# A graph attention network's gather stream: the pacing waits taken off GpSimd's gathers, and its index copies joined and moved

## The chip, the cores and the metric

One Trainium2 chip, one of its cores. The metric is the time of one execution on the device in microseconds (us); the number compared is the median over several executions. A profile is one further execution, recorded by the hardware's profiler, with a time of its own.

## The reference

A graph of 6,250 nodes with 32 channels and 106,250 directed edges (self loops among them), sorted by destination. Three GATv2 attention layers with 8 heads, each followed by a residual and a batch normalization over the nodes, then one equivariant layer and layer norms. Cut to one attention layer:

```
xl, xr = (x @ Wl + bl), (x @ Wr + br)            # [N, 8, 32]
e      = leaky_relu(xl[src] + xr[dst], 0.2)
logits = einsum('ehc,hc->eh', e, att)
p      = exp(logits - segment_max(logits, dst)[dst])
alpha  = p / (segment_sum(p, dst)[dst] + 1e-16)
out    = segment_sum(xl[src] * alpha, dst).mean(heads) + bias
x      = batchnorm(leaky_relu(out, 0.01) + x)
```

Layer 4 (the "second network") gathers wide rows of the nodes by `src`, forms messages from edge vectors and a small radial network, and adds them up by `dst`.

## The kernel before

**Steps.** The edges are cut into 468 steps of 256 edges (two columns `t` of 128, one edge on each partition), ordered so that all edges of a step belong to one block of 128 destination nodes. A step k of attention passes these stages, each on an engine with its own queue, tied by semaphores that count steps:

- GpSimd gathers the source rows by two indirect DMAs (L506), one for each column, from `table` in HBM into `xg[:, s % 6, t, 96:128]`. `xg` has six slots. The numbers of the rows lie in `idx`, a ring of 12 slots that GpSimd itself fills by small copies from `srci` (`number`, L483), one a column.
- VectorE makes the transposed one-hot `oht` of the destinations (L1150), five steps ahead of its own main work.
- TensorE's `front` (L610, L613) transposes the gathered rows into PSUM and multiplies the destination rows in by `oht`. It runs four steps ahead of TensorE's `aggregate`. ScalarE copies the result to `xt` (L830).
- TensorE's `zed` (L622, L624) multiplies by the weights, two steps ahead.
- VectorE applies the leaky relu and the attention weights (`u`, L1155), sums over channels (`lr`, L1163; this bumps `r_done`), and every third step adds the linear part to the logits (L1169).
- GpSimd's `keep_rows` (L491) copies the gathered rows of step k-3 (`LAG`) out of `xg` into `xs`, which holds two groups of rows.

**Groups.** 48 steps are a group; a layer has ten, the last with 36 steps. When a group's logits are complete, the running maxima over segments are made (`running`, `maxima`: two scans, L1257 and L1258, and a chain of short instructions between VectorE, TensorE and ScalarE). Only then can the group's rows be weighed (`px`, L1182), multiplied by a one-hot (`aggregate`, L637) and added to `acc` (L1196). This second half of group g-1 runs interleaved with the first half of group g, on the same three engines. So group 0 of a layer has only first halves, and a last stretch has only second halves. Inside `maxima` VectorE makes the one-hots of the next group's first steps (`early_places`), and TensorE their fronts (`early_fronts`), one by one between the links of the chain.

**Order on GpSimd.** `attention_body` runs 12 steps. For step k it waits that the slot is free: `front_done` of step k-6 and `xs_done` of step k-6. Before the first gather it also waits for the one-hot of step k-3 (`oht_done`, L501), before the second for the channel sums of step k-8 (`r_done`, the `else` branch, L503); before each for its own number (`idx_done`, L504). Behind each gather it copies one column's numbers for step k+1, and behind both the rows of step k-3. `then()` is a counter's increment and does no other work.

**SP** loads the destinations' places `dr` (L424) three steps at a time, once the one-hots that read the old ones are done.

Of the kernel before, what the change touches and what calls it, by code (L numbers as in the profile page):

```python
# [32 lines left out]
N, C, H, LAYERS, E = 6250, 32, 8, 3, 106250  # L33
# [5 lines left out]
S6 = 6  # L39
BODIES = 8  # L40
GS = S6 * BODIES
NBODIES = 2 * -(-(PAIRS + BLOCKS - 1) // (2 * S6))
GROUPS = -(-NBODIES // BODIES)
LASTB = NBODIES - (GROUPS - 1) * BODIES
NS = NBODIES * S6
# [14 lines left out]
ZS = SELF + NS  # L60
QS = NS // J + SELF
AGGS = NS + GROUPS + 1
NUMBERS = 2 * NS + 2
LAG = 3
AHEAD = 8
WIDE = 8 + 8 * 5
# [12 lines left out]
def gatv2_program(nc, x, src, dst, edge_w, edge_v, Wl, bl, Wr, br, att, conv_bias, gamma, beta,  # L79
# [3 lines left out]
    with ctx:  # L83
        def sb(name, shape, dt=F32):
            return ctx.enter_context(nc.sbuf_tensor(name, shape, dt))

        def sem(name):
            return ctx.enter_context(nc.semaphore(name))
# [21 lines left out]
        srci = sb("srci", [P, NSP, 2], I32)  # L110
# [20 lines left out]
        idx = sb("idx", [P, 2 * S6, 2], I32)  # L131
# [158 lines left out]
        r_done = sem("r_done")  # L290
        lin_done = sem("lin_done")
        l_done = sem("l_done")
        oht_done = sem("oht_done")
# [6 lines left out]
        idx_done = sem("idx_done")  # L300
# [160 lines left out]
        def _(pool):  # L461
# [15 lines left out]
            def then():  # L477

                pool.sem_inc(passed, 1)

            def number(k, s, t):

                nc.gpsimd.tensor_copy(idx[:, s, t:t + 1], srci[:, bass.ds(k, 1), t]).then_inc(idx_done, 1)  # L483

            rowsets = xs[:].rearrange("p g s q c -> p (g s) q c")

            def keep_rows(t, to, s):

                pool.wait_ge(gat[s], 32 * t + 32)
                then()  # L490
                nc.gpsimd.tensor_copy(to, xg[:, s, :, 96:128]).then_inc(xs_done, 1)  # L491

            def attention_body(l, i, starts):
                k0 = i * 2 * S6
                for s in range(2 * S6):

                    pool.wait_ge(front_done, AHEAD + l * ZS + k0 + s + 1 - S6)
                    pool.wait_ge(xs_done, AHEAD + l * NS + k0 + s + 1 - S6)
                    for t in range(2):
                        if t == 0:  # L500
                            pool.wait_ge(oht_done, AHEAD + l * NS + k0 + s + 1 - 3)  # L501
                        else:
                            pool.wait_ge(r_done, AHEAD + l * ZS + k0 + s + 1 - 8)  # L503
                        pool.wait_ge(idx_done, AHEAD + l * NUMBERS + (k0 + s) * 2 + t + 1)  # L504
                        then()
                        nc.gpsimd.indirect_dma_start(  # L506
                            out=xg[:, s % S6, t, 96:128], out_offset=None, in_=table,
                            in_offset=bass.IndirectOffsetOnAxis(ap=idx[:, s, t:t + 1], axis=0)).then_inc(gat[s % S6], 16)
                        number(k0 + s + 1, (s + 1) % (2 * S6), t)
                    if s >= LAG or not starts:  # L510
                        to = rowsets[:, bass.ds((k0 + (2 * GS + s - LAG)) % (2 * GS), 1), :, 0:C].rearrange("p o q c -> p (o q) c") \
                            if not starts else rowsets[:, s - LAG, :, 0:C]
                        keep_rows(l * NBODIES + i * 2 + (s - LAG) // S6, to, (s - LAG) % S6)

            pool.sem_inc(xs_done, AHEAD)
            pool.sem_inc(idx_done, AHEAD)
# [3 lines left out]
            with pool.Fori(0, LAYERS) as l:  # L520
                pool.wait_ge(x_new, l + 1)
                then()
                nc.gpsimd.memset(acc[:], 0.0).then_inc(acc_done, 1)
                for t in range(2):
                    number(0, 0, t)
                pool.wait_ge(tab_new, 16 * (l + 1))
                then()
                attention_body(l, 0, True)
                with pool.Fori(1, NBODIES // 2) as i:
                    attention_body(l, i, False)  # L530
                for s in range(S6 - LAG, S6):
                    keep_rows((l + 1) * NBODIES - 1, rowsets[:, (NS - S6 + s) % (2 * GS), :, 0:C], s)

                pool.wait_ge(f_g, l + 1)
                then()
                with pool.Fori(0, SELF // 2) as i:
                    for r in range(2):
                        m = l * SELF + i * 2 + r
                        pool.wait_ge(gb_done, AHEAD + m - 1)
                        nc.gpsimd.tensor_tensor(  # L540
                            xp[:, r].rearrange("p b (h c) -> p b h c", h=H),
                            xn[:, bass.ds(i * 4 + 2 * r, 2), :].unsqueeze(2).to_broadcast([P, 2, H, C]),
                            gate[:, 3, bass.ds(i * 4 + 2 * r, 2), :].unsqueeze(3).to_broadcast([P, 2, H, C]),
                            ALU.mult).then_inc(xp_done, 1)
# [11 lines left out]
            def numbers1(k, half):  # L556

                pool.wait_ge(pa_done, HELD + k + 3 - S6)
                nc.gpsimd.tensor_copy(idx[:, 3 * half:3 * half + 3, :], srci[:, bass.ds(k, 3), :]).then_inc(idx_done, 1)
                pool.wait_ge(idx_done, AHEAD + LAYERS * NUMBERS + k // 3 + 1)  # L560

# [1053 lines left out]
```

## Time and profile before

| | |
|---|---|
| median of 3 runs | 7,853.58 us (7,843.77 to 7,854.25) |
| the profiled execution | 7,840.21 us |
| its span, first to last instruction | 7,838.1 us |
| granted clock of TensorE, mean | 0.793 of full speed |
| GpSimd busy | 4,875.5 us, 62% |
| VectorE busy | 6,394.4 us, 82% |
| TensorE busy (matmul) | 6,163.7 us, 79% |

How to read it: PE is TensorE, PEld its weight loads, DVE VectorE, ACT ScalarE, POOL GpSimd, SP the queue that issues most loads. The three attention layers take about 1,920 us each, from 208 to 5,960 us; what follows is the equivariant layer. Busy times leave out waits on semaphores. "issue" as a releaser means that the profile shows nothing that the engine waited for. An idle time stands with the instruction behind it and with what ended it.

### The profile page before, as it was taken

The numbers are of one execution on the slowest core, as the hardware profiler recorded it, in microseconds if no ns is written. First come the engines' busy times: TensorE is split into PE (matmuls) and PEld (weight loads), VectorE is DVE, ScalarE is ACT, GpSimd is POOL, SyncE is SP. The second block draws the span as 40 slices with busy tenths as digits, with TensorE's granted clock in tenths as the row PEclk, the third lists the DMA queues.
The fourth block names the chain that finished last, engine by engine and source line by source line (L and its number), as shares of the span: only waits on it lengthen the run. The fifth ranks groups of instructions, "written<-read, shape, count | busy, mean of one in ns | idle before, by whom it ended". The sixth has DMA issues, their size and how long they took to land.

```text
span 7838.1 us, 176242 instructions
## 1 busy us (share of the span) xinstructions
PE 6163.7 (79%) x26512; PEld 4656.6 (59%) x26513; DVE 6394.4 (82%) x12894; ACT 3281.8 (42%) x11055; POOL 4875.5 (62%) x8226
## 2 busy tenths in 40 slices
PE   0688888885478888888547888888854999999998
PEld 0366666664446666655435656665544888888887
DVE  7688888885468888888547888888846999999999
ACT  0255545553125545445313545444511444444444
POOL 1888878870288878885038878887412555555554
PEclk8899999998599999999759999999965555555555
DMA  2211111110011111111001111111101111111111
GB/s 87 49 34 33 37 31 34 34 30 0 9 36 34 37 31 34 33 36 22 0 15 36 36 32 34 33 36 31 19 0 31 30 30 30 30 30 30 30 30 28
DMA packets 214500, 237.82 MB, mean 30 GB/s; under 512 B 72973, under 2 KB 195854, under 8 KB 213902
## 3 DMA queue, kind: packets, MB, share of 16 engines
q1 hardware_dynamic: 93582, 163.43, 7.2%
q0 software_dynamic: 120704, 72.40, 6.9%
q14 instruction: 185, 1.52, 0.1%
q8 instruction: 29, 0.48, 0.0%
HBM read 222.34 MB, written 13.20 MB: 30 GB/s over the span
## 4 chain that ended last, share of the span: by engine, by line
issue 27%; DVE 22%; PE 21%; POOL 12%; DVEq 11%; DMA 3%; POOLq 3%; ACT 1%; ACTq 0%; SPq 0%
POOL xg L506 7%; PE psum L637 6%; PE psum L622 6%; POOL idx L483 4%; DVE xs L1525 3%; PE psum L715 2%; DVEq L1510 2%; DVE acc L1537 2%; DMA xg<-table,idx 2%; DVEq L1189 2%; DVEq L990 2%; DVE u L1155 2%; PE psum L705 2%; PE psum L610 2%; PE psum L624 1%
## 5 line engine op out<-in xcount | busy, mean ns | idle before, releaser
L506 POOL DMA_INDIRECT xg<-table,idx x2808 | 2877.3, 1025 | 754.4 <-issue 278.0
L622 PE MATMUL psum<-wz,xt 128*128 x5928 | 1820.5, 401 | 51.2 <-ACT xt L890 49.7
L637 PE MATMUL psum<-px,oh 128*128 128x272 f32 x5616 | 1632.5, 414 | 161.2 <-DVE acc L1196 80.6
L819 ACT ACTIVATE dist<-iota_f,ndloc 128x128 f32<-128x128 f32 x2808 | 974.2, 394 | 1512.5 <-PE psum L637 1500.6
L637 PEld LDWEIGHTS psum<-px,oh 128*128 128x128 f32 x5616 | 961.7, 191 | 516.0 <-DVE acc L1196 210.8
L622 PEld LDWEIGHTS psum<-wz,xt 128*128 128x128 f32 x5928 | 1024.4, 197 | 384.6 <-ACT lin L837 72.5
L771 PE MATMUL psum<-w2e,xt 65*128 65x256 f32 x1872 | 1056.6, 668 | 228.7 <-DVE xs L1525 175.3
L552 POOL DMA_INDIRECT xg<-table,idx x936 | 905.4, 967 | 384.5 <-issue 242.2
L1163 DVE TENSOR_REDUCE lr<-u 128x16 f32<-128x512 f32 x1482 | 1012.8, 686 | 158.7 <-DVE u L1155 117.3
L1182 DVE TENSOR_TENSOR px<-xs,pg 128x528 f32 (+1 forms) x1404 | 997.1, 710 | 109.0 <-issue 47.7
L1155 DVE SCALAR_TENSOR_TENSOR u<-psum,atts 128x512 f32<-128x512 f32 x1482 | 1017.3, 686 | 71.0 <-PE psum L624 69.2
L624 PE MATMUL psum<-bz,ones_b 96*128 x2964 | 839.7, 283 | 0.0
L610 PE MATMUL psum<-ident,xg 128*128 128x128 f32 x2808 | 589.0, 293 | 263.3 <-DMA xg<-table,idx 243.5
L772 PEld LDWEIGHTS psum<-w2e,xt 65*128 65x128 f32 x1872 | 630.0, 337 | 169.0
L1196 DVE TENSOR_TENSOR acc<-acc,psum 128x272 f32 x1404 | 606.1, 432 | 121.8 <-issue 100.0
L830 ACT COPY xt<-psum 128x256 f32<-128x256 f32 x1404 | 524.1, 373 | 416.1 <-PE psum L613 252.2
L1150 DVE TENSOR_SCALAR oht<-dr,iota_p 128x256 bf16<-128x256 bf16 x1404 | 439.4, 315 | 298.7 <-PE psum L613 252.2
L483 POOL COPY idx<-srci 128x1 int32 (+1 forms) x2814 | 661.4, 235 | 16.0
L610 PEld LDWEIGHTS psum<-ident,xg 128*128 128x128 f32 x2808 | 362.0, 149 | 515.5 <-issue 339.7
L540 POOL TENSOR_TENSOR xp<-xn,gate 128x512 f32 x78 | 81.8, 1051 | 934.9 <-DVEq L990 934.9
L771 PEld LDWEIGHTS psum<-w2e,xt 65*128 65x128 f32 x1872 | 504.2, 329 | 246.2 <-DVE u L1519 183.6
L613 PE MATMUL psum<-oht,x 128*96 128x256 bf16 x1404 | 429.4, 306 | 263.4 <-issue 248.4
(270 smaller groups left out, 8379.7 us busy)
## 6 DMA issues: line engine op xcount, KB each, us to landing
dr<-dlocs SPq DMA_DIRECT2D x468, 192.0 KB
xg<-table,idx POOLq DMA_INDIRECT x3744
at<-w_rows SPq DMA_DIRECT2D x156, 192.0 KB
fl<-flags SPq DMA_DIRECT2D x30, 576.2 KB
flags<-fl SPq DMA_DIRECT2D x10, 576.2 KB, 3.1
table<-xn SPq DMA_DIRECT2D x3, 784.0 KB, 3.6
xp<-keys SPq DMA_DIRECT2D x5, 385.0 KB, 4.5
u<-keys SPq DMA_DIRECT2D x5, 385.0 KB, 4.4
```

Source lines behind the costliest of these rows:

```text
L483: nc.gpsimd.tensor_copy(idx[:, s, t:t + 1], srci[:, bass.ds(k, 1), t]).then_inc(idx_done, 1)
L506: nc.gpsimd.indirect_dma_start(out=xg[:, s % S6, t, 96:128], out_offset=None, in_=table, in_offset=bass.IndirectOffsetOnAxis(ap=idx[:, s, ...
L552: nc.gpsimd.indirect_dma_start(out=feat[:, s, e, 8:8 + WIDE], out_offset=None, in_=table1, in_offset=bass.IndirectOffsetOnAxis(ap=idx[:, s ...
L610: pe.transpose(xt_ps(r)[:, e * P:(e + 1) * P], xg[:, s, e, :], ident[:])
L622: pe.matmul(out_z, xt[:, r, e * P:(e + 1) * P], wz[:, bass.ds(l, 1), :].rearrange("p o z -> p (o z)"), start=True, stop=False)
L624: last = pe.matmul(out_z, ones_b[:], bz[:, bass.ds(l, 1), :].rearrange("p o z -> p (o z)"), start=False, stop=True)
L637: last = pe.matmul(agg_ps(r), oh[:, r, e, :], px[:, r, e, :], start=(e == 0), stop=(e == 1))
L771: pe.matmul(z_ps(r, 0, HC)[:, e, :], rows, w2e[:, 0:HC], start=True, stop=True)
L819: last = op.activation(dist[:, e, :], iota_f[:], ACT.Abs, bias=ndloc[:, bass.ds(k, 1), e])
L1155: op.scalar_tensor_tensor(u[:, r], z_ps(r, 0, HC), 0.0, atts[:, bass.ds(l, 1), :].to_broadcast([P, 2, HC]), ALU.max, ALU.mult).then_inc(u_ ...
L1163: op.tensor_reduce(lr[:, c, j], u[:, r].rearrange("p e (h c) -> p e h c", h=H), AX.X, ALU.add).then_inc(r_done, 1)
L1182: op.tensor_tensor(px[:, r, :, 0:H * C1].rearrange("p e (h c) -> p e h c", h=H), rows.unsqueeze(2).to_broadcast([P, 2, H, C1]), pg[:, 2 * ...
```

## The change

Four edits, all on GpSimd's queue and within the attention layers:

1. The two waits `oht_done` (step k-3) and `r_done` (step k-8) before the gathers are gone; a gather waits for its slot, and for the number.
2. `number` copies both columns of a step at once, 128x2 in place of 128x1, so `idx_done` counts steps and not columns (`NUMBERS`).
3. It does so for step k+2 and behind the step's second gather; the numbers of steps 0 and 1 are copied ahead of the loop.
4. `keep_rows` of step k-3 stands between the step's two gathers and no longer behind both.

```
-NUMBERS = 2 * NS + 2
+NUMBERS = NS + 2
...
-            def number(k, s, t):
+            def number(k, s):
-                nc.gpsimd.tensor_copy(idx[:, s, t:t + 1], srci[:, bass.ds(k, 1), t]).then_inc(idx_done, 1)
+                nc.gpsimd.tensor_copy(idx[:, s, :], srci[:, bass.ds(k, 1), :].rearrange("p o t -> p (o t)")).then_inc(idx_done, 1)
...
                     pool.wait_ge(front_done, AHEAD + l * ZS + k0 + s + 1 - S6)
                     pool.wait_ge(xs_done, AHEAD + l * NS + k0 + s + 1 - S6)
+                    pool.wait_ge(idx_done, AHEAD + l * NUMBERS + k0 + s + 1)
                     for t in range(2):
-                        if t == 0:
-                            pool.wait_ge(oht_done, AHEAD + l * NS + k0 + s + 1 - 3)
-                        else:
-                            pool.wait_ge(r_done, AHEAD + l * ZS + k0 + s + 1 - 8)
-                        pool.wait_ge(idx_done, AHEAD + l * NUMBERS + (k0 + s) * 2 + t + 1)
                         then()
                         nc.gpsimd.indirect_dma_start(...)
-                        number(k0 + s + 1, (s + 1) % (2 * S6), t)
-                    if s >= LAG or not starts:
-                        to = ...
-                        keep_rows(l * NBODIES + i * 2 + (s - LAG) // S6, to, (s - LAG) % S6)
+                        if t == 0 and (s >= LAG or not starts):
+                            to = ...
+                            keep_rows(l * NBODIES + i * 2 + (s - LAG) // S6, to, (s - LAG) % S6)
+                    number(k0 + s + 2, (s + 2) % (2 * S6))
...
-                for t in range(2):
-                    number(0, 0, t)
+                for s in range(2):
+                    number(s, s)
```

## Rows read from the trace of the kernel before

**Rows 1.** The page: busy time by engine; VectorE and GpSimd in 40 slices.
```profile
PE 6163.7 (79%) x26512; PEld 4656.6 (59%) x26513; DVE 6394.4 (82%) x12894; ACT 3281.8 (42%) x11055; POOL 4875.5 (62%) x8226
...
DVE  7688888885468888888547888888846999999999
...
POOL 1888878870288878885038878887412555555554
```

**Rows 2.** Waits, whole span: waiter, releaser, us in total, times, longest.
```profile
POOL xg L506 <- DVE oht L1150: 274.1, 34, 11.9
...
DVE oht L1150 <- PE psum L613: 252.2, 279, 5.2
...
PE psum L610 <- DMA xg<-table,idx: 243.5, 153, 98.3
```

**Rows 3.** Timeline of GpSimd, two steps inside a group: start, duration, instruction.
```profile
1207.29 0.97 POOL L506 DMA_INDIRECT xg<-table,idx  x1 [0.16 <-issue]
1208.26 0.19 POOL L483 COPY idx<-srci 128x1 int32 x1
1208.62 0.98 POOL L506 DMA_INDIRECT xg<-table,idx  x1 [0.16 <-POOL idx L483]
1209.60 0.20 POOL L483 COPY idx<-srci 128x1 int32 x1
1209.72 0.24 POOL L491 COPY xs<-xg 128x64 f32 x1
1210.12 0.98 POOL L506 DMA_INDIRECT xg<-table,idx  x1 [0.16 <-issue]
```

**Rows 4.** Timeline of GpSimd at two boundaries of groups, one group apart.
```profile
2450.06 0.96 POOL L506 DMA_INDIRECT xg<-table,idx  x1 [10.13 <-DVE oht L1150]
...
2607.82 0.96 POOL L506 DMA_INDIRECT xg<-table,idx  x1 [11.13 <-DVE oht L1150]
```

**Rows 5.** Waits in layer 2's groups 1 to 9 (2300 to 3672 us).
```profile
DVE oht L1150 <- PE psum L613: 34.8, 50, 2.4
...
DVE px L1182 <- POOL xs L491: 8.1, 13, 0.8
...
DVE px L1182 <- PE psum L637: 4.4, 9, 0.9
...
PE psum L610 <- DMA xg<-table,idx: 17.7, 24, 1.8
...
POOL xs L491 <- DMA xg<-table,idx: 2.1, 1, 2.1
```

**Rows 6.** Windows: busy us by engine inside a middle group; in group 0.
```profile
2461.00:2600.00 139.00, 126.59 (x605) 90.38 (x603) 122.06 (x246) 75.25 (x283) 119.71 (x223) 0.98 0.17 36
2155.30:2286.30 131.00, 93.95 (x420) 53.15 (x418) 79.41 (x156) 25.39 (x94) 115.79 (x230) 0.99 0.19 38
```

**Rows 7.** Waits in layer 2's group 0 (2150 to 2286 us).
```profile
DVE oht L1150 <- PE psum L613: 47.7, 42, 3.0
...
POOL xg L506 <- issue: 9.9, 52, 1.8
```

**Rows 8.** GpSimd in the equivariant layer: a six-column copy's group; gathers back to back.
```profile
L559 POOL COPY idx<-srci 128x6 int32 x156 | 29.1, 186 | 556.3 <-DVE u L1519 469.0 <-DVEq L1486 87.3
...
6999.04 0.96 POOL L552 DMA_INDIRECT xg<-table,idx  x1 [0.31 <-issue]
7000.31 1.05 POOL L552 DMA_INDIRECT xg<-table,idx  x1 [0.30 <-issue]
```

**Rows 9.** Durations in ns (min/median/max) in 2300 to 3672 us; groups with their means.
```profile
L483 POOL COPY idx<-srci x829: 187/195/781, 2300.9 to 3661.5; 128x1 int32 x166
...
L1150 DVE TENSOR_SCALAR oht<-dr,iota_p x416: 272/286/666, 2300.5 to 3659.9; 128x256 bf16<-128x256 bf16 x139
...
L1182 DVE TENSOR_TENSOR px<-xs,pg x419: 696/700/817, 2301.7 to 3670.6; 128x528 f32 x104, 128x528 f32<-128x528 f32 x36
...
L1182 DVE TENSOR_TENSOR px<-xs,pg 128x528 f32 (+1 forms) x1404 | 997.1, 710 | 109.0 <-issue 47.7
...
L1150 DVE TENSOR_SCALAR oht<-dr,iota_p 128x256 bf16<-128x256 bf16 x1404 | 439.4, 315 | 298.7 <-PE psum L613 252.2
```

More of the change, by code:

```diff
@@ L508, in attention_body @@
                             in_offset=bass.IndirectOffsetOnAxis(ap=idx[:, s, t:t + 1], axis=0)).then_inc(gat[s % S6], 16)
-                        number(k0 + s + 1, (s + 1) % (2 * S6), t)
-                    if s >= LAG or not starts:
-                        to = rowsets[:, bass.ds((k0 + (2 * GS + s - LAG)) % (2 * GS), 1), :, 0:C].rearrange("p o q c -> p (o q) c") \
-                            if not starts else rowsets[:, s - LAG, :, 0:C]
-                        keep_rows(l * NBODIES + i * 2 + (s - LAG) // S6, to, (s - LAG) % S6)
+                        if t == 0 and (s >= LAG or not starts):
+                            to = rowsets[:, bass.ds((k0 + (2 * GS + s - LAG)) % (2 * GS), 1), :, 0:C].rearrange("p o q c -> p (o q) c") \
+                                if not starts else rowsets[:, s - LAG, :, 0:C]
+                            keep_rows(l * NBODIES + i * 2 + (s - LAG) // S6, to, (s - LAG) % S6)
+                    number(k0 + s + 2, (s + 2) % (2 * S6))
             pool.sem_inc(xs_done, AHEAD)
```

## The prediction

> **What bounds the kernel now.** I began with the page's totals and its slices [rows 1]. In the attention layers (slices 2 to 29) GpSimd and VectorE are both busy for eight tenths and more, and TensorE has the next largest total, so no total names the bound, and the waits have to. In the waits of the whole span [rows 2], GpSimd stands 274.1 us before a gather because of a one-hot (L1150), in only 34 places; TensorE stands 243.5 us for rows that a gather has not landed, 98.3 of them once at the first layer's start; VectorE stands 252.2 us before the one-hot, because the front step (L613) of TensorE is late. So gathers are held back in one place and missed in another.
>
> The timeline of GpSimd shows where [rows 3, 4]. Between group boundaries it never rests: a step takes 2.83 us (1207.29 to 1210.12), nearly all of it two gathers and three copies. At a boundary it rests 10.13 and 11.13 us [rows 4], since a gather waits for the one-hot of three steps before, which VectorE issues only inside the running maxima. From 2450.06 to 2607.82, one group of 48 steps, GpSimd needs 157.8 - 11.1 = 146.7 us, 3.05 a step.
>
> That does not make GpSimd the bound of a whole group. In one layer's groups 1 to 9 (420 steps, 1,370 us) VectorE stood for a late front 34.8 us, and for TensorE's aggregate 4.4 us; TensorE stood for gathers 17.7 us [rows 5]. VectorE is busy 122 of 139 us in a mid-group stretch [rows 6], and most of the remaining 17 us are not the gathers' fault (34.8 / 9 = 3.9 a group is). Group 0 is different: it has no weighing and no sums, VectorE is busy 79 of 131 us and stood 47.7 us for fronts, while GpSimd's pauses before gathers are the short ones of dispatch but for one of 1.8 us [rows 6, 7]. I read this as: GpSimd sets the pace of group 0; in groups 1 to 9 VectorE does, with GpSimd so near that its lateness shows now and then.
>
> **The change part by part.**
>
> *The number copies.* Now a step is gather (0.97), copy (0.19), gap to the next gather (0.17), gather (0.98), copy, row copy that begins 0.12 later, gap: 2.83 us [rows 3]. In the trace each copy begins as the gather before it ends, and a gather begins 0.16 us after the copy before it. The new order is gather, row copy, gap, gather, one number copy, gap: 0.97 + 0.24 + 0.16 + 0.98 + 0.19 + 0.16 = 2.70. The two-column copy isn't in the trace; a copy of six columns took 186 ns against 195 for one [rows 8], so I price it as one. The saving is 0.13 us a step, not the 0.35 (0.19 and its gap) of a whole copy, because the second copy lay beside the row copy, and now each stands alone. Bounds: nothing, if the row copy waits; 0.35, if all gaps close. Nothing may close entirely: two gathers with no copy between them are still 0.30 apart [rows 8].
> In group 0 this is on the path: 48 x 0.13 = 6.2 us, in three layers 19 us (bounds 0 and 50). In groups 1 to 9 it only adds to GpSimd's lead.
>
> *The two waits.* What stays is the free slot: gather k waits for front k-6 (and the row copy, long done). TensorE runs its front four steps ahead of its own aggregate, so front k-6 is done well before the old waits end at a boundary: gathers to step 101 can go at once, while today those from 99 wait until 2450.06. That is three steps, 8.5 us of GpSimd's work, moved into the rest of 10 to 11 us. GpSimd's demand for a group falls from 146.7 to 146.7 - 48 x 0.13 = 140.5 us against a period of 157.8, so it enters with a lead near six steps and keeps most of it. A front is then late by nothing but a rare landing, so what falls away is VectorE's wait for fronts. Three layers of 34.8 make 104 us; I take 90 of it, since some of the waits may hide others that end just after (bounds 50, and 130 with 4.4 x 3 for aggregates and small pauses the view does not list). The initial 98.3 us are the layer's start and stay.
>
> *Contention.* GpSimd will work beside VectorE at other moments. What a copy can cost: the row copy is given as releaser of VectorE's product (L1182) for 8.1 us, 13 times [rows 5]; that product takes 700 ns at the median and 696 at best, the one-hot 286 and 272, with 666 at worst [rows 9]. So today's loss is near nothing for the product and at most 0.05 us a step for the one-hot. I take 5 us of loss for the 27 boundaries, where GpSimd newly works beside the scans. The bounds are a gain of 41 us (1,404 one-hots by 29 ns, what their mean of 315 lies over the median [rows 9]) and a loss of one row or number copy a step, 0.19 us. The Trainium skill, "SBUF — State Buffer" (the diagram's reading of the engine ports), has the pair of ports shared by GpSimd and VectorE as an exclusive lock: an instruction with two SBUF inputs, or in a 2-port mode, and a GpSimd instruction that reads SBUF block each other whole, and who starts first keeps the other out. The trace agrees on the direction seen from GpSimd (a number copy takes 195 ns at the median and 781 at worst) and shows almost none of it from VectorE's side. By that rule alone the saved copy could give VectorE back up to 0.19 us a step; by the product's row it gives nothing, and the sum goes by the row.
>
> *Moved past.* The row copy now stands in front of the second gather, and waits for the rows of step k-3. It does so 1.3 us sooner after their issue than today. Today it waited for a landing once in that layer's stretch, 2.1 us [rows 5], after some three steps (8.5 us); then it will be two steps and one gather (6.5 us). Behind it on GpSimd's queue stand the second gather and everything after; with six steps of lead I price it at nothing, and 2 x 3 us if the rare late ones recur. No DMA of SP is moved; its loads of places still hang on the one-hots.
>
> *Sum.* 7,840 (the profiled execution's own time; span 7,838) - 19 - 90 + 5 = 7,736. The runs' median, 7,853.6, lies 13 above the profiled one; I forecast 7,748 against it.
>
> **The rivals.**
>
> *GpSimd really sets every group's pace.* Then a group shrinks by both its rest and the copies: 157.8 to 140.5, 17 us, eight times, with 6 for group 0 and 36 x 0.13 = 5 for the last one: about 147 a layer, 441 in all, 7,412. For it: GpSimd never rests within a group, and the fronts' slack is small. Against it: VectorE, which has the maxima to do at every boundary besides its steps, stood only 3.9 us a group for fronts. Some of its other pauses might be consequences of lateness I don't see; so values between 7,650 and 7,412 belong here.
>
> *The release does nothing.* If the free slot comes no sooner than the old waits in the run of a group, and the lead taken at the boundary is lost by its middle, late fronts return in the second half. Then half of the 90 stays and group 0 gives its 19, or less: 7,854 - 19 - 15 = 7,820, with a span from 7,800 to 7,850. For it: today's lead from the boundary is used up within the group, or TensorE would not have stood for gathers 24 times in nine groups [rows 5]. Against it: GpSimd's demand, 140.5, is well under the period.
>
> *Slower: copies that block VectorE's products.* With the slots alone as release, GpSimd's step hangs on the front's end, and so keeps a fixed place against VectorE's step. If in that place the row or the number copy holds the product off for its whole length every step, it costs 1,404 x 0.19 = 267 us less the 104 gained: 8,017. It decides from 104 / 1,404 = 0.07 us a step on. The page cited above speaks for this one. Against it: at today's changing phase the product's mean is 710 ns against a median of 700 [rows 9], though GpSimd works nearly all the time, so most phases do no harm.
>
> **How the numbers follow.** The forecast has 0.66, GpSimd as the bound 0.12, a release without effect 0.13, slower 0.09. The forecast's own bounds are 7,854 - 50 - 130 - 41 = 7,633 and 7,854 - 0 - 50 + 5, about 7,810; I take 7,640 to 7,825, which also takes in half of the rival without effect and leaves the first and the last outside. A measurement of this kernel tells a difference of 0.2% (16 us) from none. Faster than that are the forecast, the first rival and some two thirds of the second, 0.86; within it the rest of the second, and a mild form of contention, 0.06; slower 0.08.
>
> **What would show it.** In the profile after, GpSimd's long waits before a gather should name the front (L613) instead of L1150; its total wait should grow to some 10 to 17 us a group, spread over it; its step without waits should be 2.70. TensorE's waits for gathers in groups 1 to 9 and VectorE's for fronts there should be near zero, and those of group 0 fall by 6 us a layer. The distance between scans (L1257), a group's period, should go from about 158 to 154. If that distance falls by over 8 us, VectorE was not the bound and the first rival holds. If L1182 or L1150 is longer, or waits for GpSimd, the last one does. If VectorE's waits for fronts vanish and the distance stays, the waits only hid something else that ends at the same moment, and my step from a wait to a gain is what fails.

## The result, and the profile after

The changed kernel takes 7,585.5 us (median of 4 runs, 7,582.3 to 7,587.4) against 7,848.7 for the kernel before beside it (7,833.2 to 7,854.3): 0.9667 of the time, 95% interval 0.9651 to 0.9684. That is 263 us less, where 105 were forecast, and outside the range of 7,640 to 7,825. The profiled execution took 7,587.1 us, span 7,585.0, at a granted clock of 0.79 as before. The times in the text on groups and steps below are worked out from starts in the traces; from the gather on, lines are lower by 4 (L506 is L502, L610 is L606, L613 is L609, L637 is L633, L1150 is L1146, L1182 is L1178, the scan L1257 is L1253).

The page after, busy time by engine and the same two rows of slices as in [rows 1]:

```profile
PE 6116.2 (81%) x26512; PEld 4596.1 (61%) x26513; DVE 6316.2 (83%) x12894; ACT 3414.8 (45%) x11055; POOL 4623.7 (61%) x6822
...
DVE  7699989985479989988458899989738999999999
...
POOL 1888878850288788873158788878013555555554
```

GpSimd is busy 252 us less, VectorE 78 less. In the attention layers VectorE's digits go from eight to nine, GpSimd's stay at eight.

Where the 253 us of the span went is told by the distances between starts: from the first to the last `u` (L1151, before L1155) of group 0, 128.1 us became 122.0, in three layers 18 us; from scan to scan, in what follows the length of a group, 158.2 became 149.3, 24 times, 213 us; the last such distance of a layer went from 138.2 to 131.0, three times, 22 us. 18 + 213 + 22 = 253.

Waits of the whole span after, as in [rows 2] (waiter, releaser, us in total, times, longest):

```profile
POOL xg L502 <- PE psum L609: 276.6, 35, 12.4
...
PE psum L606 <- DMA xg<-table,idx: 187.9, 60, 98.9
...
DVE oht L1146 <- PE psum L609: 142.2, 134, 4.9
...
POOL xs L491 <- DMA xg<-table,idx: 17.3, 7, 3.1
```

GpSimd rests as long as before (276.6 against 274.1 us) but now for the front's slot. TensorE's waits for gathers fall by 56 us, VectorE's for fronts by 110.

GpSimd's timeline after, inside a group, as in [rows 3], and at two boundaries one group apart, as in [rows 4]:

```profile
2300.08 0.98 POOL L502 DMA_INDIRECT xg<-table,idx  x1 [0.16 <-POOL idx L483]
2301.07 0.24 POOL L491 COPY xs<-xg 128x64 f32 x1
2301.47 0.98 POOL L502 DMA_INDIRECT xg<-table,idx  x1 [0.16 <-POOL xs L491]
2302.46 0.19 POOL L483 COPY idx<-srci 128x2 int32 x1
2302.81 1.38 POOL L502 DMA_INDIRECT xg<-table,idx  x1 [0.16 <-POOL idx L483]
...
2353.99 0.98 POOL L502 DMA_INDIRECT xg<-table,idx  x1 [11.12 <-PE psum L609]
...
2503.21 0.98 POOL L502 DMA_INDIRECT xg<-table,idx  x1 [11.11 <-PE psum L609]
```

A step is 2.73 us (2,300.08 to 2,302.81) where 2.70 were forecast and 2.83 were before. A group now takes 149.2 us from boundary to boundary, 11.1 of it rest: 138.1 of work, where 140.5 were forecast.

Waits in layer 2's groups 1 to 9 after (2,211 to 3,504 us), as in [rows 5]; no row there has TensorE waiting for a gather:

```profile
POOL xg L502 <- PE psum L609: 91.5, 11, 12.3
...
DVE px L1178 <- PE psum L633: 14.7, 42, 0.4
...
DVE px L1178 <- POOL xs L491: 6.6, 9, 0.8
...
POOL xs L491 <- DMA xg<-table,idx: 5.9, 3, 2.8
...
DVE oht L1146 <- PE psum L609: 0.6, 2, 0.4
```

VectorE's waits for fronts fell from 34.8 us to 0.6, as forecast; the eleven rests of GpSimd are what is left.

Windows inside a middle group and in group 0 (start:end, length, busy us of PE, PEld, DVE, ACT and POOL with their instructions, clock, DMA share, GB/s), as in [rows 6]:

```profile
2364.00:2500.00 136.00, 125.46 (x606) 86.97 (x604) 124.55 (x252) 80.36 (x281) 113.41 (x180) 1.00 0.18 37
2079.60:2195.00 115.40, 86.41 (x386) 49.68 (x384) 72.48 (x143) 23.22 (x86) 101.48 (x170) 0.97 0.20 41
```

VectorE is busy 91.6% of the stretch inside a group (87.8% before), TensorE 92.3% (91.1%), GpSimd 83.4% (86.1%). In group 0 VectorE still stands for fronts, 45.9 us between 2,060 and 2,196 us where [rows 7] has 47.7; the prediction had these waits fall by 6 us a layer.

The chain of work that ended last, cut to the same groups, is a view that the prediction doesn't use. First the kernel before (2,300 to 3,672 us), then after (2,211 to 3,504 us); the view cuts its line at the end:

```profile
by line: issue 28.6%; PE psum L637 12.2%; POOL xg L506 10.2%; PE psum L622 9.8%; POOL idx L483 6.5%; DMA xg<-table,idx 4.2%; PE psum L610 3.0%; PE psum L613 2.6%; PE psum L624 2.5%; DVEq L1189 2.1%; DVE u L1155 1.9%; POOLq L491 1.3%; DVE ac
```

```profile
by line: PE psum L633 26.2%; PE psum L618 22.3%; issue 9.4%; DVE u L1151 6.2%; PE psum L620 5.3%; PE psum L606 4.8%; DVEq L1185 3.7%; DVE acc L1192 2.5%; PE psum L609 2.4%; DVE px L1178 1.4%; DVEq L1178 1.4%; DVEq L986 1.4%; DVE oht L1146 1
```

Before, a fifth of the chain in just those groups ran through gathers, number copies and landings (10.2 + 6.5 + 4.2). After, none of the named lines is GpSimd's; TensorE's products and the path through VectorE are.

How early the rows come is a plainer test. Worked out from the traces, groups 1 to 8: from the end of a step's second gather to its front's first transpose (L610) it is never under 1.5 us in the kernel before, and 2.1 to 2.7 us at the median in 21 of a group's last 24 steps. So there the front starts almost as soon as the rows are in. After, the least of all is 8.3 us: TensorE has the rows long before it takes them.

Groups with their means after, as in [rows 9]:

```profile
L1178 DVE TENSOR_TENSOR px<-xs,pg 128x528 f32 (+1 forms) x1404 | 992.1, 707 | 95.8 <-PE psum L633 60.5 <-POOL xs L491 20.4 <-issue 8.4
...
L1146 DVE TENSOR_SCALAR oht<-dr,iota_p 128x256 bf16<-128x256 bf16 x1404 | 405.2, 290 | 181.2 <-PE psum L609 142.2 <-issue 21.7
```

### The profile page after: what moved, and what is told of

Its sections match the earlier page's. It is cut to its first block, busy times and chain, and to the rows that moved or that the text cites. A ratio compares the mean times of both kernels' runs of the same rounds, so it can differ in the third digit from the quotient of the medians.

```text
span 7585.0 us, 170428 instructions
## 1 busy us (share of the span) xinstructions
PE 6116.2 (81%) x26512; PEld 4596.1 (61%) x26513; DVE 6316.2 (83%) x12894; ACT 3414.8 (45%) x11055; POOL 4623.7 (61%) x6822
## 4 chain that ended last, share of the span: by engine, by line
PE 37%; DVE 26%; issue 18%; DVEq 14%; POOL 3%; DMA 1%; ACT 1%; POOLq 1%; ACTq 0%; SPq 0%
PE psum L633 14%; PE psum L618 12%; DVE u L1151 4%; DVE xs L1521 4%; PE psum L620 3%; DVEq L1185 3%; PE psum L711 2%; DVEq L1506 2%; PE psum L606 2%; DVE acc L1533 2%; DVEq L986 2%; DVE acc L1192 2%; PE psum L701 2%; POOL xg L502 2%; DVE u L1515 1%
## 5 line engine op out<-in xcount | busy, mean ns | idle before, releaser
L502 POOL DMA_INDIRECT xg<-table,idx x2808 | 2874.0, 1024 | 733.3 <-PE psum L609 276.6
L618 PE MATMUL psum<-wz,xt 128*128 x5928 | 1842.0, 404 | 102.7 <-ACT lin L833 51.7
L633 PE MATMUL psum<-px,oh 128*128 128x272 f32 x5616 | 1650.9, 417 | 158.5 <-DVE acc L1192 121.8
L633 PEld LDWEIGHTS psum<-px,oh 128*128 128x128 f32 x5616 | 959.6, 190 | 572.2 <-DVE acc L1192 362.2
L618 PEld LDWEIGHTS psum<-wz,xt 128*128 128x128 f32 x5928 | 966.6, 195 | 550.0 <-ACT lin L833 218.6
L1178 DVE TENSOR_TENSOR px<-xs,pg 128x528 f32 (+1 forms) x1404 | 992.1, 707 | 95.8 <-PE psum L633 60.5
L1151 DVE SCALAR_TENSOR_TENSOR u<-psum,atts 128x512 f32<-128x512 f32 x1482 | 1014.3, 684 | 68.4 <-PE psum L620 68.4
L833 ACT COPY lin<-psum 128x16 f32<-128x16 f32 x1482 | 255.2, 172 | 1316.7 <-DVE u L1151 1316.1
L606 PE MATMUL psum<-ident,xg 128*128 128x128 f32 x2808 | 579.6, 289 | 192.2 <-DMA xg<-table,idx 187.9
L606 PEld LDWEIGHTS psum<-ident,xg 128*128 128x128 f32 x2808 | 369.1, 149 | 402.8 <-issue 244.0
L819 ACT ACTIVATE oh<-dist 128x256 f32<-128x256 f32 x1404 | 585.6, 417 | 44.3
L768 PE MATMUL psum<-w2e,xt 65*128 65x128 f32 x1872 | 593.4, 421 | 0.0
```

The costliest lines, as they stand in the source:

```text
L502: nc.gpsimd.indirect_dma_start(out=xg[:, s % S6, t, 96:128], out_offset=None, in_=table, in_offset=bass.IndirectOffsetOnAxis(ap=idx[:, s, ...
L606: pe.transpose(xt_ps(r)[:, e * P:(e + 1) * P], xg[:, s, e, :], ident[:])
L618: pe.matmul(out_z, xt[:, r, e * P:(e + 1) * P], wz[:, bass.ds(l, 1), :].rearrange("p o z -> p (o z)"), start=True, stop=False)
L633: last = pe.matmul(agg_ps(r), oh[:, r, e, :], px[:, r, e, :], start=(e == 0), stop=(e == 1))
L768: last = pe.matmul(psum[:, 4 + r, e * P:(e + 1) * P], rows, w2e[:, HC:HC + P], start=True, stop=True)
L1151: op.scalar_tensor_tensor(u[:, r], z_ps(r, 0, HC), 0.0, atts[:, bass.ds(l, 1), :].to_broadcast([P, 2, HC]), ALU.max, ALU.mult).then_inc(u_ ...
```

## The experiments

Theory A was the prediction's, VectorE paces groups 1 to 9 and lateness costs what the waits show. Theory B: before, GpSimd's own time and the rest that it must take make the group; after, something else does, a floor that no group goes below. The expectations call B the lateness theory (runs 1 to 4), the theory of GpSimd's pace (5 to 8) and the floor model (from 9 on). A rival beside both is their copy theory: the second number copy slows VectorE's instructions.

**1 to 4, beside one another (the kernel before: 7,850.7 us).** The waits away alone is the kernel before less these lines:

```
-                        if t == 0:
-                            pool.wait_ge(oht_done, ...)
-                        else:
-                            pool.wait_ge(r_done, ...)
```

> The kernel before with the two pacing waits taken off the gathers, and nothing else: two number copies a step, one step ahead, the row copy behind both gathers. Lateness theory: a group of the changed kernel takes 149.3 us between scans because no front waits for rows any more; that floor belongs to VectorE and TensorE, and GpSimd meets it whenever its work and its rest at the boundary are below it. Here they are 146.7 us and a small rest, so groups 1 to 9 fall from 158.2 to 149 to 151 us, group 0 stays (first channel product to last 128 us); 7,610 to 7,650 us. Copy theory (it was the second number copy, beside VectorE's instructions, that cost the groups their time): groups stay above 154 us, 7,740 or more.

Measured: 7,681.9 us, ratio 0.9792 (0.9776 to 0.9808). A group takes 152.0 us, group 0 128.4. That is above the lateness theory's 149 to 151 and 7,650, and below the copy theory's 154 and 7,740: two copies a step cost the groups 2.7 us at most here, and neither range was met. The lead that GpSimd wins at the boundary is used up again: from the second gather's end to the front it is over 14 us in the first six steps and 2.3 in the last. The copies alone is the changed kernel with those four lines back.

> The changed kernel with both pacing waits put back: joined number copies, two steps ahead, the row copy between the gathers. Lateness theory: GpSimd needs 48 x 2.86 = 137 us and rests 11 us at the boundary, 148 together, just under the floor, so groups come to 149 to 152 us and group 0 to 122; 7,600 to 7,650 us. Copy theory: nearly the whole gain too, 7,590 to 7,620. If the waits themselves matter at every step (the free slot comes sooner than they do), groups stay at 155 or more and the time above 7,720 us.

Measured: 7,595.7, ratio 0.968 (0.9664 to 0.9696), a group 149.3, group 0 121.7, the last one 133.6. It lies 4 us under the lateness theory's range and inside the copy theory's, so this run doesn't part the two. With the new copies the release is worth some 10 us (the two ratios' intervals overlap), and the copies alone give all of the gain in groups 1 to 8. The third is the changed kernel with the row copy behind both gathers and the number copy:

```
-                        if t == 0 and (s >= LAG or not starts):
-                            ... keep_rows(...)
                     number(k0 + s + 2, (s + 2) % (2 * S6))
+                    if s >= LAG or not starts:
+                        ... keep_rows(...)
```

> The changed kernel with the row copy back behind both gathers (right behind the number copy); the rest as changed. GpSimd's step: 0.97 + 0.31 + 0.97 + 0.13 + 0.24 + 0.16 = 2.78 us against 2.70, so group 0 takes 48 x 0.08 = 4 us more a layer, and groups 1 to 9 stay at 149.3 by the lateness theory: 7,585 + 12 = 7,597 us. By the copy theory, where a copy stands matters to VectorE in each step: more than 30 us either way.

Measured: 7,611.8, ratio 0.9701 (0.9685 to 0.9717), a group 150.1, group 0 123.4. GpSimd's timeline and VectorE's one-hot in this kernel:

```profile
2300.08 0.99 POOL L502 DMA_INDIRECT xg<-table,idx  x1 [0.30 <-issue]
2301.08 0.19 POOL L483 COPY idx<-srci 128x2 int32 x1
2301.21 0.24 POOL L491 COPY xs<-xg 128x64 f32 x1
2301.60 0.98 POOL L502 DMA_INDIRECT xg<-table,idx  x1 [0.15 <-issue]
2302.89 0.95 POOL L502 DMA_INDIRECT xg<-table,idx  x1 [0.30 <-issue]
...
L1146 DVE TENSOR_SCALAR oht<-dr,iota_p 128x256 bf16<-128x256 bf16 x1404 | 478.1, 342 | 186.3 <-PE psum L609 147.5 <-issue 21.5
```

The two copies overlap here, but the gathers behind one another stand 0.30 us apart, so the step (2,300.08 to 2,302.89, gather to same gather) is 2.81 us against 2.73. And the one-hot's mean is 342 ns against 290, 1,404 x 52 ns = 73 us of VectorE's time. The kernel is 26 us slower than the changed one, of which 3 x 1.4 are group 0's; how the rest divides isn't isolated. 12 us had been expected, or over 30 by the copy theory; it is neither.

The fourth leaves the second gather of each step out, and the waits for landings count one gather a step; the second column's source rows stay zero, so that part of the attention's result is not computed.

```
-                    for t in range(2):
+                    for t in range(1):
```

> The changed kernel without its second gather in the attention steps (the second column's source rows stay zero, the output is not the reference's): GpSimd's step falls from 2.7 to about 1.5 us. Lateness theory: the floor of 149.3 us a group is VectorE's and TensorE's, so groups 1 to 9 stay within 1 us of it, and only group 0 falls, from 122 us to about 95 to 105 (TensorE was busy 94 of 131 us there): 7,500 to 7,535 us. If GpSimd still bounds the groups after the change, or its instructions slow VectorE's, they fall below 147 us, and the time below 7,470.

Measured: 7,470.8, ratio 0.9521 (0.9505 to 0.9537). A group stays at 150.0, as expected. Group 0 falls to 80.6 us, lower than the 95 to 105 expected, and with it the whole time. GpSimd's wait in this kernel, whole span:

```profile
POOL xg L502 <- PE psum L609: 1837.6, 982, 17.4
```

With half of the gathers and rests in 982 places, a group is no shorter: some 149.3 us is a floor that isn't GpSimd's, and the changed kernel stands on it. Only group 0 still hung on GpSimd.

**5 to 8 (the kernel before: 7,867.9 us).** In the kernel before, TensorE has idle time with no releaser ("issue") just before L613, where the block number is loaded into a register behind the wait for a gather. Rows of the kernel before, then of after, in the stretches of [rows 5]:

```profile
PEld psum L613 <- issue: 114.7, 217, 1.0
...
PE psum L613 <- issue: 60.2, 141, 0.7
```

```profile
PEld psum L609 <- issue: 15.8, 51, 0.8
...
PE psum L609 <- issue: 2.5, 7, 0.4
```

The fifth loads the number ahead of the wait, in the kernel before, and the eighth does in the changed one (the fronts at a group's start excepted):

```
+                b = pe.value_load(brow[0:1, bass.ds(k, 1)], ...)
                 pe.wait_ge(gat[s], 32 * t + 32)
...
-                b = pe.value_load(brow[0:1, bass.ds(k, 1)], ...)
```

> The kernel before, and in TensorE's front the load of the block number stands ahead of the wait for the gathered rows (but for the early fronts), not between the transposes and the one-hot's matmul. Before, TensorE stood 60 us a layer before that matmul (L613) for nothing that the profile names, in groups 1 to 9, and the changed kernel 2.5 us. Theory of GpSimd's pace: those pauses only fill time until the next rows land; a group lasts as long as GpSimd's work plus its rest (145.7 + 11.7 = 157.4 us), whatever TensorE does in it; the time falls by no more than 25 us. Theory of the exposed load: late rows cost the time of a load that the sequencer can no longer do ahead, 6.4 us a group; then it falls by 100 to 170 us, to 7,680 to 7,750.

Measured: 7,833.7, ratio 0.9957 (0.9941 to 0.9974), 34 us less, where 25 at most were expected by the theory of GpSimd's pace and 100 by the other; a group 157.9, and the profiled span 9 us less than before's. TensorE's waits in this kernel, in the same stretch of 2,300 to 3,672 us (the gather's wait is at L612, the one-hot's product at L616):

```profile
PE psum L612 <- DMA xg<-table,idx: 75.6, 106, 2.1
...
PE psum L616 <- issue: 2.5, 7, 0.4
```

Before, the two rows were 17.7 [rows 5] and 60.2, 77.9 in sum; now 75.6 and 2.5, 78.1 in sum. A group shrank by 0.4 us. The "issue" before L613 had been the gather's lateness under another name.

> The changed kernel with the same early load of the block number in TensorE's front. Rows are 5.6 us early there in groups 1 to 8, so nothing waits for the load in them: 7,585 us, within 10. If TensorE bounds the changed groups (it has the largest share of the chain that ended last, 37%), it may fall by 20 us or more.

Measured: 7,582.0 (7,579.3 to 7,583.8), ratio 0.9636 (0.962 to 0.9652); a group 149.3, group 0 120.8. Of the kernels that compute the whole result it is the fastest, but only 3 us under the changed kernel, beside a kernel before that took 19 us more; nothing to tell apart.

The sixth has the joined numbers two steps ahead alone (waits kept, rows behind both gathers); the seventh only moves the row copy between the gathers, in the kernel before.

> The joined number copies, two steps ahead, and nothing else: both pacing waits kept, the row copy behind both gathers (behind the number copy). GpSimd's step with the waits gone and this order was 2.87 us (active 2.56 and a gap of 0.31 between gathers). Theory of GpSimd's pace: 48 x 2.87 + 11.7 = 149.5 us a group, so 150 to 151; with group 0 at 123 us 7,615 to 7,650 us in all. If the place of the row copy is what gives the gain, it stays above 7,750 us.

Measured: 7,615.8, ratio 0.9679 (0.9663 to 0.9695), a group 150.1, group 0 123.7.

> The kernel before, with the row copy moved from behind both gathers to between them (behind the first column's number copy); both number copies and both waits kept. GpSimd's step: still two gathers, a lone number copy and a pair of number and row copy, 2.83 us. Theory of GpSimd's pace: no change, within 20 us of before. If the place of the row copy matters by itself (it meets VectorE elsewhere), more than 50 us.

Measured: 7,873.7, ratio 1.0003 (0.999 to 1.0015), a group 159.9. So the joined copy, two steps ahead, carries the change; its two parts were not tried apart. The row copy's place is worth nothing by itself. Where the numbers are joined it is worth 26 us between run 3 and after, and 20 between runs 6 and 2, whose ratios are the same, so that this second one isn't shown.

**9 to 18: more GpSimd work, and less.** If B holds, copies that nobody reads (`spare`) bring the old group time back, in proportion, once GpSimd's work passes the floor. One and three such copies a step:

```
                     number(k0 + s + 2, (s + 2) % (2 * S6))
+                    for c in range(3):
+                        nc.gpsimd.tensor_copy(spare[:, c, s, :], srci[...])
```

> The changed kernel with one number copy more in each step, written where nobody reads it. Where the chip does not pause (the kernel before at about 7,850 us): if GpSimd's active time sets a group once it passes the floor of 149.3 us, 48 steps of 2.86 + 0.35 (a copy of 0.19 and its gap of 0.16) are 154 us, so a group takes 154 to 156 us, group 0 about 135 to 139, and the time is 7,585 + 24 x 6 + 3 x 15 + 3 x 6, about 7,790 us. If VectorE sets the groups and GpSimd counts only for late rows now and then, the group stays within 2 us of 149.3 and only group 0 grows, 7,630 us.

Measured (the kernel before: 7,858.7): 7,629.6, ratio 0.9711 (0.9694 to 0.9727). A group takes 150.2 us, group 0 127.5. The spare copy started 0.13 us after the number copy (median) and cost GpSimd 0.19 us a step, not 0.35, so that its work stayed under the floor. The expectation priced the copy wrong, and the number came out as if VectorE alone counted; by itself this run doesn't part the theories of pace. It does settle the copy theory: with two copies of numbers a step again, a group is 0.9 us longer and not 8.9.

> The changed kernel with three number copies more in each step, written where nobody reads them. Where the chip does not pause: if GpSimd's active time sets the group, 48 steps of about 3.35 us (as this kernel had on the chip that pauses) make 161 us a group and about 138 in group 0: 7,585 + 24 x 12 + 3 x 16 + 3 x 10, about 7,950 us, slower than the kernel before. If the floor of 149.3 us holds, 7,640 us. On a chip that pauses it takes about 8,100 us again, and less than the changed kernel there.

Measured: 7,954.3, ratio 1.0123 (1.0106 to 1.014). A group takes 161.9 us, group 0 138.2, as expected to 4 us in the whole. Slower instructions of VectorE can't be the reason: it is busy 137.9 us a group here and 134.8 after, 3.1 of the 12.6 us. The chain in its layer 2's groups 1 to 9 (2,354 to 3,768 us):

```profile
by line: issue 38.2%; PE psum L636 7.8%; PE psum L621 6.8%; POOL spare L512 6.3%; POOL xs L492 6.2%; POOL xg L503 6.0%; POOL idx L484 3.6%; DMA xg<-table,idx 2.8%; PE psum L609 2.0%; PE psum L612 1.7%; PE psum L623 1.7%; POOLq L492 1.6%; DV
```

Copies that nobody reads are on the path, 6.3%, and the same instructions of GpSimd as in the kernel before are back. The time from a gather's end to the front falls from 15 us at a group's start to 2 within half of it, and its least is 1.5 us, as before.

From the traces, for groups 1 to 8: GpSimd's rest (its pauses of over 0.3 us before gathers, in the early load and numbers only of over 0.32), and its active time, which is the distance from a group's first gather to the next one's, less the rest. The last column is the distance between scans:

| kernel | old waits | active, us a step | x 48 | rest | group |
|---|---|---|---|---|---|
| before | yes | 3.036 | 145.7 | 11.7 | 158.2 |
| early load (run 5) | yes | 3.047 | 146.2 | 11.1 | 157.9 |
| rows between only | yes | 3.070 | 147.4 | 11.9 | 159.9 |
| numbers only | yes | 2.893 | 138.9 | 10.5 | 150.1 |
| copies only | yes | 2.853 | 136.9 | 11.6 | 149.3 |
| waits away only | no | 3.062 | 147.0 | 4.4 | 152.0 |
| one spare copy | no | 3.044 | 146.1 | 3.4 | 150.2 |
| three spare copies | no | 3.344 | 160.5 | 0.9 | 161.9 |
| after | no | 2.856 | 137.1 | 10.7 | 149.3 |

Work and rest add up to about the group in every row by their definition, after's too, where GpSimd doesn't set the pace; so the sum proves nothing. What the table shows is the rest. With the old waits it stays at 10.5 to 11.9 us whatever the copies cost. Without them it gives way, to 4.4 and 3.4 us near the floor and to 0.9 above it. That a group with the old waits is the work plus that rest, or the floor if that is higher, fits the five rows; in two of them the two amounts lie within 1 us of each other.

These two kernels, one with less GpSimd work, and the changed kernel itself had run twice before that, on chips in a condition in which the kernel before took 8,577.8 and 8,583.5 us; the second of these chips was that of runs 5 to 8. All expected times, meant for a kernel before at 7,850 us, were missed there by over 100 us.

> The changed kernel with one more copy of the step's numbers, into a tile that nobody reads, behind the number copy: GpSimd's step grows by the 0.13 us at which a second copy starts behind a first. Floor model: a group takes the larger of 149.3 us and GpSimd's work and rest; 48 x (2.86 + 0.13) = 143.5 plus a rest of 4 to 10 us is 148 to 153, so groups rise by 0 to 3 us, group 0 by 48 x 0.13 = 6 us; 7,585 + 19 + (0 to 75) = 7,604 to 7,680. A cost of copies by contention with VectorE would show in its one-hot's and product's lengths, and in groups above 151 us with fronts still early.

> The changed kernel with one spare copy a step (as in the run before with it; there the kernel before took 8,578 us, and every engine, in the untouched last layer too, paused for what the profile does not name). Floor model: 7,604 to 7,680 us, groups 149 to 152 us, where the kernel before takes about 7,850.

Measured: 8,452.6 and 8,453.0, ratios 0.9855 (0.9838 to 0.9871) and 0.9849 (0.9831 to 0.9868).

> The same with three spare copies, 0.39 us a step: 48 x 3.25 = 156 us and a rest of about 4.4 us (that of the kernel without pacing waits and with the old copies) make 160 us a group, 11 above the floor, group 0 takes 19 us more: 7,585 + 24 x 11 + 3 x 19 + 3 x 10 for the last groups = 7,936 us, give or take 40. If GpSimd's time is not what sets a group above the floor, it stays below 7,750.

> Three spare copies a step. Floor model: GpSimd's 48 x 3.35 us (measured active time a step in the first such run) plus a rest of about 1 us make 161 to 163 us a group, group 0 takes 138 us; 7,585 + 24 x 13 + 3 x 16 + 3 x 7 = 7,966 us, give or take 30. If GpSimd's time is not what sets a group above the floor, under 7,750.

Measured: 8,113.8 and 8,098.7, ratios 0.9457 (0.9441 to 0.9473) and 0.9437 (0.9419 to 0.9455); a group 162.3 and 161.8, the length expected of it.

The number copy of six steps at once, every sixth step (128x12 numbers), with the early load of run 8:

```
-                    number(k0 + s + 2, (s + 2) % (2 * S6))
+                    if s % S6 == LAG:
+                        number(k0 + s + LAG, (s + LAG) % (2 * S6))
```

> The changed kernel with the early load of the block number, and the numbers of six steps copied at once (128x12), every sixth step. GpSimd's step: 0.97 + 0.24 + 0.16 + 0.97 + 0.31 = 2.65 us and a sixth of a copy, some 0.04 under 2.70. Groups 1 to 8 are at the floor already, so only group 0 and the end of the last group gain: 5 to 15 us under the changed kernel, 7,570 to 7,580. If copies cost VectorE time by contention, more.

> The changed kernel with the early load in TensorE's front and the numbers of six steps copied at once: 5 to 15 us under the changed kernel beside it, 7,570 to 7,580 us.

Measured: 8,480.5 and 8,475.6, ratios 0.9882 (0.9865 to 0.9898) and 0.9869 (0.9843 to 0.9894).

> The changed kernel itself, run beside the three others on one chip: 7,585 us, its ratio to the kernel before 0.967.

> The changed kernel itself beside the three others: 7,585 us, ratio 0.967 where the chip runs the kernel before in 7,850 us.

Measured: 8,488.9 and 8,488.8, ratios 0.9892 (0.9876 to 0.9909) and 0.989 (0.9871 to 0.991); a group 175.5 and 175.9. Whether six steps at once beat one is untested where nothing pauses; groups 1 to 8 stand on the floor there, so that little but group 0 could gain.

## Why the prediction was wrong

**Group 0.** Right in its length and cause: 6.2 us a layer were forecast and 6.1 measured; with the waits alone away it stays (128.4), with the copies alone it falls (121.7). VectorE's waits for fronts were to fall by as much and fell by 1.8, so they were no measure of the gain here either.

**The pace of groups 1 to 9: the step that failed.** "I read this as: GpSimd sets the pace of group 0; in groups 1 to 9 VectorE does, with GpSimd so near that its lateness shows now and then." With it fell the sum's 90 us "of VectorE's wait for fronts": 235 were measured (213 + 22). The prediction's own test, a distance between scans that falls by over 8 us, came out at 8.9. What failed is the sentence behind it too: "most of the remaining 17 us are not the gathers' fault (34.8 / 9 = 3.9 a group is)", said of the time in which VectorE is idle. No reason was given for the other 13. Of the 8.9 us, VectorE's busy time gave 3.0 (137.7 to 134.8 a group), its idle time the other six.

What the runs showed in its place: GpSimd sets the pace before. Rows reach TensorE just in time there and 8.3 us early after; a lighter stream of copies with the old waits still in place takes a group to 149.3 (run 2), and a heavier one without them to 161.9 (run 16). The prediction's "demand" of 146.7 us could not tell this, as it was the period less the rest, 157.8 - 11.1, and such a sum equals the period in any kernel. "GpSimd's demand, 140.5, is well under the period" held the demand of after against the period of before.

The view that misled is the waits. An engine that is late by a little delays its consumers by a little each time, and each of them shows it under another name. From start to start, TensorE's last L610 to L613 fell inside a group from 0.353 to 0.127 us, in 44 steps 9.9 us, which the waits call "issue"; run 5 shows what that was. On VectorE, the 47 steps inside a group went from 138.6 to 130.0: 4.1 us between the sum (`acc`) and the next one-hot, 1.5 between `acc` and the logits, 0.8 between logits and one-hot, the rest in five smaller ones. The 3.9 us a group of the wait row lie among these.

**The first rival.** "GpSimd really sets every group's pace" had the mechanism with a chance of 0.12, but its number, 7,412, let the group fall to 140.5. The floor of 149.3 was missing. Runs 2 and 4 show the floor, run 16 that GpSimd's work sets the group above it, once the rest is used up (0.9 us).

**The two waits.** The release was to give nearly all, the copies nothing in groups 1 to 9 ("it only adds to GpSimd's lead"). Alone, the release gives 169 us and the copies 255; together 263. The copies take the groups to the floor, so that the release behind them buys hardly anything; the release alone leaves them 2.7 us above it, and group 0 where it was. The rival "the release does nothing" was near to the truth, 10 us, beside the copies; alone it was wrong. Its sum doesn't come out either: half of the 90 kept and group 0's 19 are 64 us of gain, 7,790, where it has 34 and 7,820. The rests didn't spread over the group: they stayed at the boundaries, 11.1 us.

**Contention.** A loss of 5 us was taken, bounds a gain of 41 and a loss of a copy a step. VectorE's one-hot went from 439.4 to 405.2 us in all, 34 of the 41, and the product from 710 to 707 ns. How much of the 34 lies in the 253 isn't isolated. The slower rival fell: the products during which a copy of GpSimd ran for 150 ns or more took 706 ns in the mean, those with no copy beside them 705 (after, from the trace), and the longest of all took 834 against 696 at best. The Trainium skill, "SBUF — State Buffer" (the diagram's reading of the engine ports), has the two engines block each other whole; by the product's rows no sign of it, by the one-hot's, 290, 315 or 342 ns with the place of the copies, a small one.

**The row copy.** It waits for landings 17.3 us against 7.2, but the rows are used 8.3 us or more after the gather's end in groups 1 to 8, so that it is off the path there. What it costs in group 0 no run isolates.

What the floor is made of stays open. TensorE's and VectorE's busy shares inside a group, 92% and 92%, don't decide between them, and no run shortened either one's work.

## What to carry to other kernels

An engine that does not rest between two forced rests is a suspect for the bound, however small the waits on it are. Its work plus its rest, both taken from the trace, always equal the period and prove nothing. Look instead at how long its results lie ready before they are used, and whether that lead is at its least; read the chain of that stretch alone; and give the engine a little more work, to see if the period grows. Then estimate the next limit as well, or the rival with the right mechanism gives the wrong number. And an "issue" gap on an instruction just behind a wait can belong to the wait: move the register load ahead of it and look where the time goes.

## What the runs showed of the hardware

Two indirect gathers back to back lie 0.30 us apart, and 0.16 apart from a copy between them, so that a short copy there (0.19 to 0.24 us) costs GpSimd a tenth of a microsecond or less. A copy behind a copy starts 0.13 us after it at the median (0.12 in run 16, where four stand in a row) and overlaps it. A 128x2 number copy takes 217 ns in the mean after, a 128x1 one 234 before. TensorE takes a step's rows 1.4 us after the second gather's end at the earliest (run 5; 1.5 in the kernel before).

One thing stays unexplained. In the condition with the kernel before at 8,580 us, engines pause for reasons the profile has no name for, or calls "remote", GpSimd up to 2.7 us at a time. Waits of the changed kernel there (the last run of all in that condition), whole span:

```profile
POOL xg L502 <- issue: 472.1, 2265, 2.2
...
POOL xg L502 <- remote: 418.6, 275, 2.6
...
DVE oht L1146 <- remote: 325.9, 183, 11.5
```

No row of the changed kernel's first trace is called "remote". The untouched equivariant part, from the last `u` of the attention layers to the end, takes 2,223 to 2,232 us there against 2,096, whichever kernel runs. But the attention layers end at 6,264 us with the changed kernel (5,489 before that) and at 5,866 with three spare copies (5,864). With three spare copies the attention layers hardly paused (GpSimd's waits of the name "remote" went from 425.5 and 418.6 us to 0.2 and 1.5), so that the kernel with more work was 390 us faster than the one with less. It was seen on both chips; why is open. So the gain of this change holds where nothing pauses, 3.3%, and is 1.1% where the chip does.
